# Cosines and key casts read from PSUM, a norm root written to PSUM, and the order of the norm, the maxima and the exponentials in a fused two-layer FFN block

## The reference

```python
def rotary_xpos(q, k):
    q = q * cos * scale + rotate_half(q) * sin * scale
    k = k * cos / scale + rotate_half(k) * sin / scale
    return (q, k)

def _layer(x, wqkv, qs, ksc, wo, lg, lb, w1, b1, w2, b2):
    h = shift_token(x)
    q, k, v = jnp.split(h @ wqkv, 3, axis=-1)      # 8 heads of 64
    q = l2norm(q) * qs
    k = l2norm(k) * ksc
    q, k = rotary_xpos(q, k)
    o = local_attention(q, k, v)                   # window 64, softmax
    x = x + o @ wo
    h = shift_token(x)
    mu = h.mean(-1, keepdims=True)
    var = h.var(-1, keepdims=True)
    h = (h - mu) / jnp.sqrt(var + 1e-05) * lg + lb
    a, g = jnp.split(h @ w1 + b1, 2, axis=-1)
    return x + (a * gelu(g)) @ w2 + b2
...
x = x + 0.5 * ffn(layernorm(x))      # DEPTH = 2 layers
x = x + attn(layernorm(x))
x = x + 0.5 * ffn(layernorm(x))
```

## Time and profile before

| what | us |
|---|---|
| median of 3 runs (2467.78 to 2474.09) | 2468.51 |
| the profiled execution | 2465.03 |
| its span in the trace | 2462.9 |
| busy in the span: PE / DVE / ACT / POOL | 2116.9 / 1809.3 / 1462.6 / 1058.3 |
| first FFN block, about | 69 to 862 |
| second FFN block, about | 1277 to 2070 |

### The profile page before, as it was taken

The page is one execution under the profiler, slowest core; times in us unless marked ns, Lnnn a source line. Parts: engine busy times, 40 slices in busy tenths (PEclk is TensorE's granted clock), DMA queues, the critical chain, the costliest instruction groups (busy, mean ns, idle before and its releaser), DMA issues. The chain is left out here.

```text
span 2462.9 us, 56322 instructions
## 1 busy us (share of the span) xinstructions
PE 2116.9 (86%) x23398; PEld 1565.7 (64%) x23398; DVE 1809.3 (73%) x2815; ACT 1462.6 (59%) x2389; POOL 1058.3 (43%) x800
## 2 busy tenths in 40 slices
PE   2799999998989868999868999999989997597968
PEld 1566666666666645555536667676666664495758
DVE  3688888888888646777727888888888884563556
ACT  0477776766666515666546776766666674363635
POOL 4665555545555210000035565655555450550245
PEclk8799999999999968999979999999999998698979
DMA  7000000079999995000000000000000003121122
GB/s 151 1 2 1 2 2 2 1 78 105 111 137 129 126 127 51 2 2 2 2 1 1 2 2 2 2 2 2 2 2 2 1 2 76 54 66 37 35 75 80
DMA packets 211376, 90.91 MB, mean 37 GB/s; under 512 B 79700, under 2 KB 206721, under 8 KB 210996
## 3 DMA queue, kind: packets, MB, share of 16 engines
q1 hardware_dynamic: 202596, 72.27, 24.5%
q0 software_dynamic: 6080, 11.76, 1.5%
q10 hardware_dynamic: 2448, 3.28, 0.6%
HBM read 24.31 MB, written 63.41 MB: 36 GB/s over the span
## 5 line engine op out<-in xcount | busy, mean ns | idle before, releaser
L490 POOL TENSOR_TENSOR work<-work,rot_tables 128x512 f32<-128x512 f32 x256 | 382.6, 1515 | 317.3 <-ACT work L594 317.3
L498 POOL TENSOR_TENSOR work<-work 128x1024 f32<-128x1024 f32 x128 | 304.8, 2381 | 283.6 <-DVE work L924 278.4
L941 DVE TENSOR_TENSOR work<-work,small 128x1024 f32<-128x1024 f32 x128 | 234.4, 1833 | 56.6 <-ACT small L608 50.1
L924 DVE TENSOR_TENSOR work<-work,rot_tables 128x1024 f32<-128x1024 f32 x128 | 219.3, 1713 | 11.6 <-ACT work L594 11.6
L1081 DVE TENSOR_REDUCE small<-psum 128x4 f32<-128x1024 f32 x128 | 156.6, 1223 | 90.3 <-PE psum L1582 88.5
L1482 PE MATMUL psum<-centered,ffn_w 128*128 128x256 f32 x768 | 191.2, 401 | 3.0 <-DVE centered L985 2.9
L705 ACT ACTIVATE work<-psum 128x1024 f32<-128x1024 f32 x128 | 131.0, 1024 | 88.7 <-PE psum L1582 88.4
L1323 PE MATMUL psum<-qkv_w_hi,h_hi 128*128 128x512 f32 x384 | 180.0, 469 | 2.2 <-ACT work L594 2.2
L1420 PE MATMUL psum<-work 64*128 64x128 f32 (+1 forms) x2048 | 178.9, 304 | 0.0
L1482 PEld LDWEIGHTS psum<-centered,ffn_w 128*128 128x128 f32 x768 | 146.0, 197 | 31.2 <-DVE centered L985 4.4
L1453 PE MATMUL psum<-work,v 128*32 128x192 f32 (+1 forms) x4096 | 164.8, 302 | 0.0
(11 more groups left out here) (279 smaller groups left out, 5266.1 us busy)
## 6 DMA issues: line engine op xcount, KB each, us to landing
h_area<-mean_weights SPq DMA_DIRECT2D x24, 2048.0 KB
tile_x<-h_area SPq DMA_DIRECT2D x39, 128.5 KB, 2.1
stage<-in_consts ACTq DMA_DIRECT2D x1, 2817.0 KB, 12.0
tile_x<-h_area SPq DMA_DIRECT2D x39, 64.5 KB, 1.8
work<-in_x SPq DMA_DIRECT2D x4, 512.0 KB, 27.2
expert_w<-in_ew SPq DMA_DIRECT2D x1, 2048.0 KB, 8.4
expert_w<-in_ew SPq DMA_DIRECT2D x8, 256.0 KB, 6.6
work<-y_tokens SPq DMA_DIRECT2D x4, 512.0 KB, 6.1
```

The lines of the kernel that those rows point to most:

```text
L490: last = pool.tensor_tensor(b[:, :, :, o_], a[:, :, :, i_], tab[:, l, 1, t, :, o_].unsqueeze(2).to_broadcast([P, 2, HEADS, 32]), ALU.mult)
L498: pool.tensor_tensor(rC[:, t, :], rC[:, t, :], rB[:, t, :], ALU.add).then_inc(f_sum, 1)
L924: dve.tensor_tensor(g(rC[:, t, :]), g(rA[:, t, :]), tab[:, l, 0, t, :, :].unsqueeze(2).to_broadcast([P, 2, HEADS, DH]), ALU.mult)\
L941: dve.tensor_tensor(c_, c_, sm[0][:, 96 + 16 * t:112 + 16 * t].unsqueeze(2).to_broadcast([P, 16, DH]), ALU.mult).then_inc(f_nrm, 1)
```

## The change

`cosines` reads q and k from PSUM instead of from `rA`, so it waits for the projection (`f_qk`) and no longer for the copy. `copy_qk` in its turn waits for `cosines` of the same half. In DVE's order `cosines(i,0)` goes up behind `k_out`, and `cosines(i,1)` stands ahead of `m_out`. `k_out` makes both its outputs from PSUM. `rstd` writes its Exp to PSUM, over the variance, and `y_normed` reads it there; `y_normed` goes ahead of `m_split`, and `m_T` on PE waits for `y_normed`. On ACT `copy_v` goes ahead of `copy_qk(i,1)`, and two of the three `exps` ahead of `rnorm`. On PE two of the three groups of masks of `scores` no longer wait for `copy_qk(i,0)`. On POOL `rotated` is two instructions of half the size.

```diff
@@ -495,7 +495,10 @@
                 def rotated(i, t):
                     pool.wait_ge(f_sin, 2 * i + t + 1)
                     pool.wait_ge(f_cos, 2 * i + t + 1)
-                    pool.tensor_tensor(rC[:, t, :], rC[:, t, :], rB[:, t, :], ALU.add).then_inc(f_sum, 1)
+                    for h in range(2):
+                        n_ = slice(h * INNER, (h + 1) * INNER)
+                        last = pool.tensor_tensor(rC[:, t, n_], rC[:, t, n_], rB[:, t, n_], ALU.add)
+                    last.then_inc(f_sum, 1)
 
                 def normed(s):
                     n = f * SEQS + s
@@ -587,8 +590,7 @@
 
             def ffn(f):
                 def copy_qk(i, t):
-                    act.wait_ge(f_qk, 3 * i + t + 1)
-                    free(act, f_cos, 2 * i + t - 1)
+                    act.wait_ge(f_cos, 2 * i + t + 1)
                     free(act, f_sin, 2 * i + t - 1)
                     src = PS[:, 1 + t:3 + t, :]
                     act.activation(rA[:, t, :].rearrange("p (b n) -> p b n", b=2), src, ACT.Copy).then_inc(f_cp, 1)
@@ -634,7 +636,7 @@
                 def rstd(i):
                     act.wait_ge(f_var, i + 1)
                     link(act.activation(ysq[:, :], PS[:, 7, T:2 * T], ACT.Ln, bias=eps[:, 0:1]))
-                    act.activation(ysq[:, :], ysq[:, :], ACT.Exp, scale=-0.5).then_inc(f_rstd, 1)
+                    act.activation(PS[:, 7, T:2 * T], ysq[:, :], ACT.Exp, scale=-0.5).then_inc(f_rstd, 1)
 
                 def gelu(i):
                     l, _ = layer_of(i)
@@ -668,18 +670,20 @@
                         square(i - 2)
                         rstd(i - 2)
                     if new:
+                        copy_v(i)
                         copy_qk(i, 1)
-                        copy_v(i)
                         square_qk(i, 1)
                     if old:
                         gelu(i - 2)
                     if pre:
                         x_square(n)
+                    if mid:
+                        exps(i - 1, 0)
+                        exps(i - 1, 1)
                     if new:
                         rnorm(i)
                     if mid:
-                        for q in range(3):
-                            exps(i - 1, q)
+                        exps(i - 1, 2)
                     if mid:
                         recips(i - 1, 0)
                     if pre:
@@ -907,8 +911,8 @@
             def ffn(f):
                 def k_out(i):
                     dve.wait_ge(f_kT, i + 1)
-                    link(dve.tensor_copy(in_halves(kT), by_half(PS[:, 5:7, :])))
-                    dve.tensor_copy(kb[:, :, :], kT).then_inc(f_kb, 1)
+                    dve.tensor_copy(in_halves(kT), by_half(PS[:, 5:7, :]))
+                    dve.tensor_copy(in_halves(kb[:, :, :]), by_half(PS[:, 5:7, :])).then_inc(f_kb, 1)
 
                 def o_norm(i, a):
                     dve.wait_ge(f_o, 2 * i + a + 1)
@@ -919,9 +923,9 @@
                 def cosines(i, t):
                     l, _ = layer_of(i)
                     g = lambda x: x.rearrange("p (g h d) -> p g h d", g=2, h=HEADS)
-                    dve.wait_ge(f_cp, 2 * i + t + 1)
+                    dve.wait_ge(f_qk, 3 * i + t + 1)
                     free(dve, f_qT, i)
-                    dve.tensor_tensor(g(rC[:, t, :]), g(rA[:, t, :]),
+                    dve.tensor_tensor(g(rC[:, t, :]), PS[:, 1 + t:3 + t, :].rearrange("p g (h d) -> p g h d", h=HEADS),
                                       tab[:, l, 0, t, :, :].unsqueeze(2).to_broadcast([P, 2, HEADS, DH]), ALU.mult)\
                         .then_inc(f_cos, 1)
 
@@ -982,7 +986,7 @@
 
                 def y_normed(i):
                     dve.wait_ge(f_rstd, i + 1)
-                    dve.tensor_tensor(ycen[:, :], ycen[:, :], ysq[:, :], ALU.mult).then_inc(f_norm, 1)
+                    dve.tensor_tensor(ycen[:, :], ycen[:, :], PS[:, 7, T:2 * T], ALU.mult).then_inc(f_norm, 1)
 
                 def gated(i):
                     l, _ = layer_of(i)
@@ -1019,6 +1023,8 @@
                         o_norm(i - 2, 1)
                     if mid:
                         k_out(i - 1)
+                    if new:
+                        cosines(i, 0)
                     if old:
                         resid(i - 2)
                     if mid:
@@ -1028,16 +1034,16 @@
                     if mid:
                         s_max(i - 1, 1)
                         s_max(i - 1, 2)
-                        m_split(i - 1)
                     if old:
                         y_normed(i - 2)
+                    if mid:
+                        m_split(i - 1)
                     if new:
-                        cosines(i, 0)
+                        cosines(i, 1)
                     if mid:
                         m_out(i - 1)
                     if new:
                         sums(i, 0)
-                        cosines(i, 1)
                     if old:
                         gated(i - 2)
                     if new:
@@ -1381,10 +1387,11 @@
                 def scores(i):
                     pe.wait_ge(f_kb, i + 1)
                     pe.wait_ge(f_qsb, i + 1)
-                    pe.wait_ge(f_cp, min(2 * i + 3, 2 * ITEMS * (f + 1)))
                     groups = (((3, 6), range(8), P, 0, 0, ms0), ((4, 5), range(4), J0W, 1, WIN, ms1),
                               ((0, 1), range(4, 8), J0W, 1, WIN, ms1))
                     for bs, hs, w, _, _, m in groups:
+                        if bs[0] == 0:
+                            pe.wait_ge(f_cp, min(2 * i + 3, 2 * ITEMS * (f + 1)))
                         bands(bs, len(hs) // 2, w, m)
                     for bs, hs, w, t, k0, _ in groups:
                         for h in hs:
@@ -1395,7 +1402,7 @@
 
                 def m_T(i):
                     pe.wait_ge(f_mlo, i + 1)
-                    free(pe, f_rstd, i)
+                    free(pe, f_norm, i)
                     pe.wait_ge(o_rstd, min(f * SEQS + i % ITEMS + 3, SEQS * (f + 1)))
                     for t in range(TILES):
                         last = pe.matmul(PS[:, 7, t * P:(t + 1) * P], mneg[:, t, :], eyeb[:, :],
```

## The result

| what | us |
|---|---|
| after, median of 4 runs (2552.04 to 2563.57) | 2554.6 |
| before, runs beside it, median (2467.78 to 2474.09) | 2468.85 |
| ratio, 95% interval | 1.0349 (1.032 to 1.0379) |
| the profiled execution of after, its span | 2554.74, 2552.6 |
| busy in the span: PE / DVE / ACT / POOL | 2126.2 / 1701.4 / 1483.9 / 957.8 |

The account below looks back on a forecast made before the run. DVE, late in mid-step before, gives way to ACT's chain as the bound (0.83). 28 early steps at 1.5 us and 36 others at 1.3 make 89, taken as 87: 2465.0 becomes 2552, median 2555; range 2515 to 2605.

Parts of the forecast that it names:

- The chain: ACT from second copy (behind `cosines(i,1)`) through squares and `gelu` to `gated`, `x_center`, `attend`: `attend` 1.2 us later, at 21.3.
- Part 1: Head of a step: first copy of q and k stands behind `k_out` and `cosines(i,0)`; products of `scores` start 0.8 us later.
- Part 2: `y_normed` ahead of the split: `m_T` starts at 11.2, 1.5 us later; root read from PSUM and Exp into PSUM, no change.
- Part 4, early steps: Tail from `attend` to next `qk_T`, with `rnorm` behind two `exps`: early step 25.7 us against 24.22, +1.5 us.
- What the moved `exps` bring: Ahead of `attend`: `rnorm` no longer between `x_square` and `exps`, saving its 0.8 us less the 0.33 of `x_square`.
- Part 4, late steps: Late step's tail: `rnorm` 2.7 us later, first `qk_norm` gives back 1.45; step of 24.08 us grows by 1.3.
- The relief of DVE: Rival: DVE sheds work and PE's waits ahead of `attend` and in `qk_T` go; 61 us faster, 2408; chance 0.04.
- Absorbed: Rival: PE's 1.5 us of delays fall into its waits of 0.91 and 1.02 us; 35 us slower, 2503; chance 0.04.
- the third rival: More PE waiting lowers the granted clock, at 0.95 in both blocks 64 us more, 2620; chance 0.09.
- At most a fixed part: Halved `rotated` on POOL costs at most a fixed part, where POOL waits for DVE and ACT: nothing.

Follow-up runs that it names:

- the last run: Changed kernel with three parts undone together: second copy ahead of its cosine product and `copy_v`, keys cast from SBUF, `rnorm` ahead of all `exps`; 2429.39 us, ratio 0.9826.
- The run with waits of 2.50 us in each late step: Kernel before with `cosines(i,1)` reading PSUM right behind `cosines(i,0)`, third group of `scores_T` waiting for it, POOL's sum whole; 2520.75 us, ratio 1.019.

## Why the prediction held, and where its steps did not

The time was 2555 forecast and 2554.6 measured. The mechanism was right. The sum of 87 us is made of terms of which two were off and others were missing, and that the total came within a microsecond is luck, as the sizes below show.

**The chain.** Right, and shown: turning the second copy and its cosine product round gives 80 us back. Its points, forecast and measured as offsets from `qk_T` (372.04): second copy 12.4 and 12.25; table load ahead of `gelu` 14.55 and 14.38; end of `gated` 17.5 and 17.52; end of `x_center` 19.2 and 19.18; `attend` 21.3 and 21.30.

**Part 1** held: the key cast took 1.22 us (my upper value was 1.23), the cosines from PSUM 1.22, the first copy waited 1.34 us, and the third group of masks started 5.60 us in against 5.62. The two runs on the cast show why it is a price: 0.42 us a step behind it in the changed kernel, nothing in the kernel before.

**Part 2** held: `m_T` at 11.14 against 11.2. The root from PSUM cost nothing, 0.42 us against 0.43, and the Exp into PSUM took 0.39 us against 0.42. The Trainium skill, page "VectorE: DVE Perf Modes", section on the TRN2 errata, would make a PSUM source 65 ns longer; these rows disagree.

**Part 4, early steps: too small.** I forecast 25.7 us and measured 26.39. From `attend` to `qk_T` I took the 4.16 us of the kernel before, in which PE does not wait, and added 0.2 to 0.3 for the turn of q. It is 398.43 - 393.34 = 5.09 us. The step that failed is the one that followed the late `rnorm` only to `o_norm`, which does end when I forecast it (25.85 us in against 25.9): between them stands `resid2`, and PE's `x_var` waits for it, 0.88 us, ahead of the second half of `attend`. "What the moved `exps` bring" was therefore counted without what they take. They are a loss of 0.8 us in each early step of the kernel before and of 0.45 in the changed one.

**Part 4, late steps: too large.** Forecast +1.3, measured +1.07. The first `qk_norm` started 20.4 us into the step against 20.6, the 0.2 us by which ACT's chain came earlier, and took the 1.23 us that I forecast.

**Missing: the fill.** I took only 2 us off for the first and last steps of both blocks. The first step became 4.2 us shorter in each block, from one `k_out` to the next. Up to `attend` it is 1.6 us shorter (18.21 us instead of 19.78), with DVE late in the kernel before. The other 2.7 us lie behind `attend`, where PE does the same work in 4.16 us instead of 6.83. Before:

```profile
103.82 1.29 PE L1445 MATMUL psum<-work,ones 128*32 128x192 f32 x16 [3.87 <-ACT work L622]
104.88 2.36 PE L1453 MATMUL psum<-work,v 128*32 128x192 f32 x32
```

and after:

```profile
104.12 0.75 PE L1452 MATMUL psum<-work,ones 128*32 128x192 f32 x16 [1.07 <-ACT work L624]
104.68 1.27 PE L1460 MATMUL psum<-work,v 128*32 128x192 f32 x32
```

Behind its wait of 3.87 us PE ran at the lower level of its clock (granted 0.50 from 103.8 to 109.4 us), behind the one of 1.07 us at the upper (1.00). So most of this gain is the clock, and it is not sure to come: in the run with two `exps` moved in the kernel before, PE waits 3.39 us there in both blocks, and the first step takes 27.25 us in one and 23.52 in the other.

**The sum.** The 24 full early steps were forecast 16 us too cheap (2.15 against 1.5 us each). The 36 others cost 8 us less than forecast (1.07 to 1.1 against 1.3), and the two first steps gave back 8 that I had not counted. Two more terms were not in the forecast at all: the 4.5 us of the two steps near 700 us and the 4.5 us ahead of the blocks and between them. The two profiled executions lie 90 us apart, the medians 86.

**The rivals.** The relief of DVE is real, as the late steps of the last run show (1.3 us shorter than before), but it needed the second copy to start before 10.7 us and it started at 12.25. Absorbed: no, what PE waits for came later too. The clock stayed at 1.00 from 560 to 660 us at a busy share of 0.88, and fell for some 8 us only, near 700 us, behind the gap shown above, so the third rival stayed small. The run with waits of 2.50 us in each late step had more of it.

**POOL's halves.** "At most a fixed part" was right here, but my reason, that POOL waits for others anyway, was the wrong question. What matters is which small DVE instruction starts while POOL works. The kernel before has such a row in its first step, the clip beside POOL's `sines`, two of 3.47 us together that end at 100.87 (the clip at 100.91), and I had not read it:

```profile
99.70 1.21 DVE L935 TENSOR_SCALAR small<-small 128x32 f32<-128x32 f32 x1
```

## What to carry to other kernels

Reading PSUM directly relieves an engine only if the copy that frees the bank does not then stand behind the reader: ask of each pair "who reads, who copies" which of the two heads the longer chain, and let that one go first. When a step on one engine is moved, walk its queue to the next engine that waits for anything behind it, not only to the instruction you have in mind. And a change that costs time as a whole can hold a gain: undo its parts one by one, and keep those that don't cost.
